# One table of experts' rows for all blocks: 17 whole tiles, then 22 of the other rows

## The chip, the core and the metric

The kernel runs on one core of a Trainium2 chip, as one launch. Its engines each have their own queue of instructions: TensorE (PE; its weight loads are PEld), VectorE (DVE), ScalarE (ACT), GpSimd (POOL) and SyncE (SP), which here issues transfers. They meet only in semaphores. The metric is the device time of a whole execution in microseconds.

## What is computed

A decoder layer in float32 over 32 sequences of 64 tokens with 256 features, in three parts, each added to its input after a layer norm: self-attention, cross-attention to a context, and a feed-forward layer of experts. The last is what the change is about (routing is computed on the normalized input):

```
probs = softmax(x @ Wr)                      # 2048 tokens, 8 experts
topk_w, topk_idx = top_k(probs, 2)
topk_w = topk_w / sum(topk_w)
for i in range(8):
    w_i = sum(topk_w * (topk_idx == i))
    h = silu(x @ Wg[i]) * (x @ Wu[i])        # 256 -> 256
    output = output + w_i * (h @ Wd[i])      # 256 -> 256
```

## The kernel before

Every engine has one Python function that writes its instructions in order (`tensor`, `vector`, `scalar`, `gpsimd`, `sync`). The self-attention runs in eight chunks by a table of due times; cross-attention in four blocks of 512 tokens. Neither is changed, but the routing of a block is done inside the work of the next one, and the routing of the last block (3) inside the expert stage.

Experts are computed only for the rows that chose them. There are 2 x 2048 rows (a token goes to two experts). Each normalized token row is written twice by an indirect transfer on GpSimd (`scatter`, eight for each block, line 1832) into a table in memory, `slots`, at expert base + position within the expert. The table is filled before with rows that name an unused place. Then tiles of 128 rows are read back (`load`, SP, line 1944), one expert each. A tile step i does this:

- TensorE: `gate_up(i)` (six products of 512 columns, three per half of the features, since each float32 is split in a high and a low part), `h_T(i-1)` (transposes of the gated product), `down(i-2)` (six of 256 columns), `x_T(i+2)` (transposes of the tile after next), and then the step's part of the routing, if any.
- VectorE: `gated(i)` writes gu (line 1458), `h_low(i-1)` writes thl (1462), `x_low(i+2)` writes txl (1445), `places(i+2)` writes place (1453), the rows of the results to write to; then the routing's part, the table's part or a `combine`.
- ScalarE: `silu(i)` writes sg, `h_high(i-1)` thh, `copy_out(i-2)` ys, `x_high(i+2)` txh.
- GpSimd: `store(i)` writes ys by an indirect transfer to `results` (line 1866).
- SP: `load(i+6)`; later `results_load(t)`, which brings the two result rows of 128 tokens to gb (line 1953), and `result`, which writes the output.

`h_T(i)` waits for gu of tile i and for thl of tile i-1, `gate_up(i)` for txl of tile i. There are four buffers xs for tiles, six ys and four gb.

The number of tiles is fixed when the kernel is built, for the worst case of a routing. Blocks 0 to 2 have a table of their own: 3072 rows, 24 tiles and up to 7 more since each expert's last tile may be part full, 31. Block 3 has the other: 8 + 7 = 15. From the counts per expert VectorE works out, on all partitions alike, which expert and which first row each tile has (`table_ends`, `table_rows`, lines 1289 to 1311): compare the tile number with the running ends, sum the gaps passed. TensorE and SP read these numbers into registers, eight tiles at a time.

The routing of block 3 stands in the tile steps given by `ROUTE_LAST`: statistics in step 0, normalizing in 2, transposes in 4, logits and maximum in 6, exponential in 8, rank in 9 and 10, choice in 11, shares in 12, positions in 13, slots in 14. The second table follows in steps 15 and 16, and tile 31 is the first that needs it. The combines (two instructions on VectorE for 128 tokens, line 1469) of the first 12 token tiles need the results of all 31 tiles and stand from step 38 on, one a step.

## Times and profile before

| | |
|---|---|
| median of three runs | 696.07 us (695.46 to 696.71) |
| the profiled execution | span 694.2 us from its first to its last instruction; its own run time is not given separately |
| TensorE busy | 636.9 us (92% of the span) |
| VectorE, ScalarE, GpSimd busy | 501.9, 349.2, 256.0 us |
| chain that ended last, by engine | TensorE 79%, ScalarE 8%, VectorE 8%, issue 3%, DMA 2% |
| stores of expert tiles on GpSimd | 46, of 965 ns each |
| loads of tiles, of results | 46 of 129 KB, 16 of 256 KB |
| fill of the two tables | 13416 and 5160 KB, landing after 53.5 and 61.5 us |
| expert stage | gated products from 557.6 to 676.7 us |
| TensorE's granted clock from 560 to 680 us | 1.00 |

The chain is followed back from the last instruction: at each step to what released it. What stands on it costs time; an engine that is busy beside it costs none. "Idle before" of an instruction is in square brackets in a timeline, with what ended it.

### The profile page before, as it was taken

The page shows a single profiled execution, that of the slowest core. Times are in us where ns is not written, and L with a number is a line of the kernel's source. Part 1 is how long each engine was busy: PE and PEld are TensorE (multiplying, and loading weights), DVE is VectorE, ACT ScalarE, POOL GpSimd, SP SyncE. Part 2 cuts the span into 40 slices and gives each one's busy share as a digit, 9 for nine tenths or more (in the row PEclk, how much of TensorE's full clock was granted, in tenths as well). Part 3 has the DMA queues.
Part 4 walks back from the last instruction along what each step waited for, and adds up shares of the span by engine and source line. Part 5 has one row for each costly group of instructions (what it writes and reads, how often), then busy time and mean ns, then how long its engine had stood idle before and what let it go on. Part 6 is the DMA issues. An engine that isn't in the chain of part 4 may idle for free.

```text
span 694.2 us, 15360 instructions
## 1 busy us (share of the span) xinstructions
PE 636.9 (92%) x5650; PEld 474.0 (68%) x5650; DVE 501.9 (72%) x1210; ACT 349.2 (50%) x1207; POOL 256.0 (37%) x233
## 2 busy tenths in 40 slices
PE   3787999998899999999999999999989899999991
PEld 2456777777778667675676766776746688888881
DVE  4998989997468786647986488864788865745585
ACT  1367989997581115721267012670337755455550
POOL 2104000000005744733366642765436322454331
PEclk9998999997799999999999999999998999999996
DMA  8699990000000000000000300003045123344467
GB/s 289 165 373 304 333 319 2 2 2 2 1 1 17 16 1 3 1 16 1 1 2 1 101 23 1 2 10 100 0 149 165 54 77 89 111 124 130 132 195 244
DMA packets 42008, 61.77 MB, mean 89 GB/s; under 512 B 15280, under 2 KB 36272, under 8 KB 41328
## 3 DMA queue, kind: packets, MB, share of 16 engines
q1 hardware_dynamic: 36528, 49.23, 23.7%
q0 software_dynamic: 3744, 10.26, 4.0%
q10 hardware_dynamic: 1664, 1.31, 0.7%
q8 instruction: 46, 0.75, 0.5%
q14 instruction: 26, 0.21, 0.1%
HBM read 48.44 MB, written 31.38 MB: 115 GB/s over the span
## 4 chain that ended last, share of the span: by engine, by line
PE 79%; ACT 8%; DVE 8%; issue 3%; DMA 2%; POOL 0%; ACTq 0%; another core or an unknown queue 0%; SPq 0%; POOLq 0%; DVEq 0%
PE bank L362 68%; PE bank L371 11%; ACT kbd L1546 2%; DMA lncol<-in_L_attn_ln_kv_b 1%; ACT vbd L1532 1%; DVE wlo L1403 1%; ACT ex L1556 1%; ACT xth L1512 1%; DMA gb<-results 1%; ACT ex L1672 1%; DVE m L1122 0%; DMA results<-ys,place 0%; DVE xhat L1362 0%; DVE x L1469 0%; ACT wbh L1602 0%
## 5 line engine op out<-in xcount | busy, mean ns | idle before, releaser
L1122 DVE TENSOR_TENSOR m<-bank,cst 128x512 f32<-128x512 f32 x192 | 122.0, 684 | 38.4 <-PE bank L362 37.1
L1818 POOL TENSOR_TENSOR r<-m,m 128x512 f32<-128x512 f32 x80 | 104.5, 1330 | 114.5 <-DVE m L1122 95.1
L1672 ACT ACTIVATE ex<-bank,nmax 128x64 f32<-128x64 f32 x256 | 73.1, 338 | 27.3 <-DVE nmax L1369 27.3
L362 PE MATMUL bank<-xth,wbh 128*128 128x512 f32 x192 | 79.9, 416 | 1.1 <-DVE m L1122 1.1
L362 PE MATMUL bank<-xth,wbl 128*128 128x512 f32 x192 | 75.2, 392 | 0.0
L362 PE MATMUL bank<-xtl,wbh 128*128 128x512 f32 x192 | 75.1, 391 | 0.0
L1655 ACT ACTIVATE qc<-bank 128x512 f32<-128x512 f32 x32 | 17.4, 595 | 102.6 <-PE bank L362 102.6
L1866 POOL DMA_INDIRECT results<-ys,place x46 | 44.4, 965 | 64.1 <-ACT ys L1745 57.3
L362 PE MATMUL bank<-wop,qc 128*128 128x256 f32 x256 | 62.5, 389 | 0.0
L362 PE MATMUL bank<-r,wqk 64*64 64x512 f32 x512 | 57.7, 594 | 0.0
L362 PEld LDWEIGHTS bank<-wop,qc 128*128 128x128 f32 x256 | 46.4, 189 | 15.2 <-issue 8.8
L1556 ACT ACTIVATE ex<-bank,nmax 128x64 f32<-128x64 f32 x256 | 54.3, 360 | 1.6 <-DVE nmax L1024 1.5
L1672 ACT ACTIVATION_READ_ACCUMULATOR ex<-bank,nmax 128x1 f32 x216 | 49.6, 230 | 0.0
L362 PEld LDWEIGHTS bank<-xth,wbh 128*128 128x128 f32 x192 | 36.0, 188 | 19.0 <-issue 10.1
L1783 POOL TENSOR_TENSOR x<-x,borow 128x512 f32<-128x512 f32 x8 | 10.1, 1270 | 104.9 <-DVE xhat L956 79.4
L1838 POOL TENSOR_TENSOR ex<-ex,inv 128x512 f32<-128x512 f32 x32 | 33.4, 1044 | 41.0 <-DVE inv L1379 40.6
L371 PE MATMUL bank<-cst,ex 128*128 128x128 f32 x256 | 42.6, 291 | 5.8 <-ACT ex L1556 3.3
L371 PEld LDWEIGHTS bank<-cst,ex 128*128 128x128 f32 x256 | 30.2, 147 | 19.1 <-issue 8.8
L362 PEld LDWEIGHTS bank<-xth,wbl 128*128 128x128 f32 x192 | 36.0, 188 | 8.1
L362 PE MATMUL bank<-whi,txh 128*128 x92 | 40.3, 438 | 1.0 <-DVE wlo L1403 1.0
L362 PEld LDWEIGHTS bank<-xtl,wbh 128*128 128x128 f32 x192 | 36.1, 188 | 6.4
L362 PEld LDWEIGHTS bank<-r,wqk 64*64 64x64 f32 x512 | 18.7, 133 | 31.7 <-issue 31.7
(222 smaller groups left out, 1492.1 us busy)
## 6 DMA issues: line engine op xcount, KB each, us to landing
slots<-in_fill SPq DMA_DIRECT2D x1, 13416.0 KB, 53.5
xs<-slots SPq DMA_DIRECT2D x46, 129.0 KB
slots<-in_fill SPq DMA_DIRECT2D x1, 5160.0 KB, 61.5
gb<-results SPq DMA_DIRECT2D x16, 256.0 KB
wo_s<-in_L_xattn_Wo SPq DMA_DIRECT2D x1, 2048.0 KB, 18.6
wq_s<-in_L_xattn_Wq SPq DMA_DIRECT2D x1, 2048.0 KB, 11.8
wraw<-in_L_ffn_Wg SPq DMA_DIRECT2D x8, 256.0 KB, 3.8
wraw<-in_L_ffn_Wu SPq DMA_DIRECT2D x8, 256.0 KB, 3.9
```

Source lines behind the costliest of these rows:

```text
L362: return e.matmul(o, l, r, start=start, stop=stop, skip_group_check=True)
L371: last = e.transpose(o, i, ident)
L1122: last = e.tensor_tensor(m4[n % 2][m][:, :].rearrange("p (b s) -> p b s", s=S), products[half][:, :].rearrange("p (b s) -> p b s", s=S), t ...
L1403: e.tensor_tensor(wlo[:, at], wraw[:, at], whi[:, at].bitcast(F32), ALU.subtract).then_inc(w_lo, 1)
L1546: last = e.activation(kbd[p2][:, :, 2 * t:2 * t + 2, 64 * h2:64 * h2 + 64], bank[0][:, 256:512].rearrange("p (t b l) -> p t b l", t=2, b=2 ...
L1556: last = e.activation(ex[u][:, h * 64:(h + 1) * 64], bank[3 + u % 2][:, h * 64:(h + 1) * 64], ACT.Exp, bias=nmax[u][:, h:h + 1], scale=1.0)
L1655: e.activation(qc[:, 2 * g + pair, :], latent_banks(blk, g)[pair][:, :], ACT.Copy).then_inc(c_qb, 1)
L1672: last = e.activation(ex[b % 4][:, h * 64:(h + 1) * 64], score_banks(b)[odd][:, n * 64:(n + 1) * 64], ACT.Exp, bias=nmax[b % 4][:, 4 * odd ...
L1783: e.tensor_tensor(two, two, borow[:, :].rearrange("p (o d) -> p o d", o=1).broadcast_to([P, 2, D]), ALU.add).then_inc(s_xb, 1)
L1818: last = e.tensor_tensor(rope[n % 6][half][:, :], m4[n % 2][first][:, :], m4[n % 2][second][:, :], op)
L1838: e.tensor_tensor(segments(ex[b % 4]), segments(ex[b % 4]), per_head(inv[b % 2]), ALU.mult).then_inc(c_exn, 1)
L1866: e.indirect_dma_start(out=results[:, :], out_offset=bass.IndirectOffsetOnAxis(ap=place[:, i:i + 1], axis=0), in_=ys[i % YS][:, :], in_off ...
```

## The change

All four blocks now share one table with 2048 rows of room for each expert. After block 2 only whole tiles are certain to be complete: 3072 rows of which at most 127 for each expert are left over, at least 17 whole tiles. These 17 are the first part. What remains of the first three blocks and all of block 3 are the second part of 22 tiles, with 16 entries (expert and blocks) instead of 8; the tiles of the early entries come first in it, so the first three blocks' rows are complete after 31 tiles (`EARLY_DONE`), as before. Together 39 tiles. The routing of block 3 has to be done before tile 17, so it stands in steps 0 to 8, its tables in steps 9 and 10, its scatters in front of stores 7 to 10, two each. Combines begin at step 35, two a step. The constants in SBUF grow (`le` 64 to 256 columns, `next` 16 new, `ebase` 16 to 8, `fill` 12 to 22, `iota` 31 to 22). The table of rows in memory has 17408 rows in place of 13312 + 5120.

```diff
 WE = 2 * KD * F + KF * D
-PARTS_OF = ((0, 3), (3, 4))
-CAP = [4 * P * (hi - lo) for lo, hi in PARTS_OF]
-TILES = [2 * c // P + E - 1 for c in CAP]
+EARLY = 3
+CAP = NT * P
+WHOLE = -(-(2 * 4 * P * EARLY - E * (P - 1)) // P)
+TILES = [WHOLE, 2 * NT + E - 1 - WHOLE]
 FIRST = [0, TILES[0]]
 COLS = [0, -(-TILES[0] // 8) * 8]
+EARLY_DONE = (2 * 4 * P * EARLY + E * (P - 1)) // P
 YS = 6
-ROWS = [-(-(E * c + (E - 1) * P) // 512) * 512 for c in CAP]
+ROWS = -(-(E * CAP + (E - 1) * P) // 512) * 512
...
         RK = 26
+        TAB = 7
         ROUTE_AT = {"stats": 6, "norm": 7, "T": 9, "logits": 10, "max": 10, "exp": 11, "rank": 11, "pos": 12, "slots": 13}
         AHEAD = 6
-        ROUTE_LAST = {"stats": 0, "norm": 2, "T": 4, "logits": 6, "max": 6, "exp": 8, "rank": 9, "pos": 13, "slots": 14}
-        RANK_PARTS = 4
-        COMBINE_AT = TILES[0] + 7
+        ROUTE_LAST = {"stats": 0, "norm": 1, "T": 2, "logits": 3, "max": 3, "exp": 4, "rank": 5, "pos": 7, "slots": 8}
+        LAST_SCATTERS = {7: (0, 1), 8: (2, 3), 9: (4, 5), 10: (6, 7)}
+        COMBINE_AT = EARLY_DONE + 4
...
-                if b in (0, 3):
+                if b == 0:
...
+                n = CAP // P
+                count = pos_bank(b)[:, 64:64 + E].rearrange("p (n o) -> p n o", o=1)
+                if b == EARLY - 1:
+                    e.tensor_tensor(whole[:, :, :], count.broadcast_to([P, E, EARLY * 4]), in_tiles(C("fill")[:, 1:1 + EARLY * 4], E), ALU.is_ge)
+                e.tensor_tensor(full[:, :, :], count.broadcast_to([P, E, n]), in_tiles(C("fill")[:, 0:n], E), ALU.is_gt).then_inc(r_route, 1)
...
+            def early_table():
+                n = TILES[0]
+                w.wait_ge(r_route, RK * EARLY)
+                e.tensor_reduce(nwhole[:, :], whole[:, :, :], AX, ALU.add)
+                e.memset(starts[:, 2 * E:2 * E + 1], float(E * CAP))
+                e.tensor_reduce(early[:, :], full[:, :, :], AX, ALU.add).then_inc(r_tab, 1)
+                w.wait_ge(r_tab, 1)
+                e.tensor_scalar(gap[:, 0:E], nwhole[:, :], -float(P), float(CAP), ALU.mult, ALU.add)
+                e.scalar_tensor_tensor(starts[:, E:2 * E], early[:, :], float(P), C("ebase"), ALU.mult, ALU.add)
+                upto_of(nwhole[:, :], E)
...
+                past_of(n, E)
+                w.wait_ge(r_tab, 4)
+                e.tensor_copy(used[:, 0:1], taken[:, 0:1])
+                e.tensor_tensor(used[:, 1:E], taken[:, 1:E], taken[:, 0:E - 1], ALU.subtract)
+                e.tensor_scalar(own[:, 0:n], C("iota")[:, 0:n], float(P), C("part"), ALU.mult, ALU.add)
+                e.tensor_reduce(expert[:, 0:n], past[:, 0:n, 0:E], AX, ALU.add)
...
+                e.tensor_tensor(own[:, 0:n], own[:, 0:n], rowf[:, 0:n], ALU.add)
+                e.tensor_tensor(row[:, 0:n], C("fill")[:, 0:n], rowf[:, 0:n], ALU.add).then_inc(r_tab, 1)
+                w.wait_ge(r_tab, TAB)
+                e.drain().then_inc(r_table, 1)
+
+            def late_ends():
+                w.wait_ge(r_route, RK * 4)
+                w.wait_ge(r_tab, TAB)
+                e.tensor_reduce(early[:, :], full[:, :, :], AX, ALU.add).then_inc(r_tab, 1)
+                w.wait_ge(r_tab, TAB + 1)
+                e.scalar_tensor_tensor(stops[:, E:2 * E], early[:, :], float(P), C("ebase"), ALU.mult, ALU.add).then_inc(r_tab, 1)
+                w.wait_ge(r_tab, TAB + 2)
+                e.tensor_tensor(spans[:, E:2 * E], stops[:, E:2 * E], starts[:, E:2 * E], ALU.subtract)
+                e.tensor_tensor(gap[:, :], starts[:, 1:2 * E + 1], stops[:, :], ALU.subtract).then_inc(r_tab, 1)
+                w.wait_ge(r_tab, TAB + 3)
+                e.tensor_scalar(spans[:, E:2 * E], spans[:, E:2 * E], 1.0 / P, None, ALU.mult).then_inc(r_tab, 1)
+                w.wait_ge(r_tab, TAB + 4)
+                upto_of(spans[:, :], 2 * E)
+                w.wait_ge(r_tab, TAB + 5)
                 e.tensor_reduce(ends[:, :], upto[:, :, :], AX, ALU.add).then_inc(r_tab, 1)
-                w.wait_ge(r_tab, at + 3)
-                number = C("iota")[:, 0:n].rearrange("p (n o) -> p n o", o=1).broadcast_to([P, n, E])
-                e.tensor_tensor(past[:, 0:n, :], number, in_tiles(ends[:, :], n), ALU.is_ge).then_inc(r_tab, 1)
-
-            def table_rows(q):
-                n, at = TILES[q], 10 * q
-                mine = slice(FIRST[q], FIRST[q] + n)
-                w.wait_ge(r_tab, at + 4)
-                e.tensor_scalar(own[:, mine], C("iota")[:, 0:n], float(P), C("part"), ALU.mult, ALU.add)
-                e.tensor_reduce(expert[:, 0:n], past[:, 0:n, :], AX, ALU.add)
-                e.tensor_tensor(pastgap[:, 0:n, :], past[:, 0:n, :], in_tiles(gap[:, :], n), ALU.mult).then_inc(r_tab, 1)
-                w.wait_ge(r_tab, at + 5)
-                e.tensor_scalar(eoff[:, COLS[q]:COLS[q] + n], expert[:, 0:n], float(E - 1), float(WE), ALU.min, ALU.mult)
-                e.tensor_reduce(rowf[:, 0:n], pastgap[:, 0:n, :], AX, ALU.add).then_inc(r_tab, 1)
-                w.wait_ge(r_tab, at + 6)
-                e.tensor_tensor(own[:, mine], own[:, mine], rowf[:, 0:n], ALU.add).then_inc(r_tab, 1)
-                e.scalar_tensor_tensor(row[:, COLS[q]:COLS[q] + n], C("iota")[:, 0:n], float(P), rowf[:, 0:n], ALU.mult, ALU.add).then_inc(r_tab, 3)
-                w.wait_ge(r_tab, at + 10)
+                w.wait_ge(r_tab, TAB + 6)
+                past_of(TILES[1], 2 * E)
+            def late_rows():
+                n, cols = TILES[1], slice(COLS[1], COLS[1] + TILES[1])
+                mine = slice(FIRST[1], FIRST[1] + n)
+                w.wait_ge(r_tab, TAB + 7)
+                e.tensor_scalar(own[:, mine], C("iota"), float(P), C("part"), ALU.mult, ALU.add)
+                e.tensor_tensor(pastnext[:, :, :], past[:, :, :], in_tiles(C("next"), n), ALU.mult)
+                e.tensor_tensor(pastgap[:, :, :], past[:, :, :], in_tiles(gap[:, :], n), ALU.mult).then_inc(r_tab, 1)
+                w.wait_ge(r_tab, TAB + 8)
+                e.tensor_reduce(expert[:, :], pastnext[:, :, :], AX, ALU.add)
+                e.tensor_reduce(rowf[:, :], pastgap[:, :, :], AX, ALU.add).then_inc(r_tab, 1)
+                w.wait_ge(r_tab, TAB + 9)
+                e.tensor_scalar(eoff[:, cols], expert[:, :], float(WE), None, ALU.mult)
+                e.scalar_tensor_tensor(own[:, mine], rowf[:, :], starts[:, 0:1], own[:, mine], ALU.add, ALU.add)
+                e.scalar_tensor_tensor(row[:, cols], rowf[:, :], starts[:, 0:1], C("fill"), ALU.add, ALU.add).then_inc(r_tab, 1)
...
+                    rank_sum(b)
                 elif b == 3 and n == at["rank"] + 1:
-                    rank_sum(b)
-                elif b == 3 and n == at["rank"] + 2:
                     rank_chosen(b)
-                elif b == 3 and n == at["rank"] + 3:
                     rank_shares(b)
...
-                    table_ends(1)
+                    late_ends()
-                    table_rows(1)
+                    late_rows()
                 if i >= COMBINE_AT:
-                    combine(i - COMBINE_AT)
-            for t in range(tiles + 2 - COMBINE_AT, NT):
+                    for t in range(2 * (i - COMBINE_AT), 2 * (i - COMBINE_AT) + 2):
+                        combine(t)
+            for t in range(2 * (tiles + 2 - COMBINE_AT), NT):
                 combine(t)
...
-                t, half = divmod(i - ROUTE_LAST["slots"], 3)
-                if 0 <= t < 4 and half < 2:
+                for n in LAST_SCATTERS.get(i, ()):
                     w.wait_ge(t_hT, i + 2)
-                    scatter(3, 2 * t + half)
+                    scatter(3, n)
                 store(i)
...
-            for n, d in enumerate(slots):
-                rows = a["fill"][sum(ROWS[:n]):sum(ROWS[:n + 1]), :]
-                e.dma_start(d.rearrange("(p n r) d -> p n (r d)", p=P, r=4), rows.rearrange("(p n r) d -> p n (r d)", p=P, r=4)).then_inc(d_fill, 16)
+            e.dma_start(slots.rearrange("(p n r) d -> p n (r d)", p=P, r=4), a["fill"].rearrange("(p n r) d -> p n (r d)", p=P, r=4)).then_inc(d_fill, 16)
...
-                w.wait_ge(d_scat, 128 * PARTS_OF[q][1])
+                w.wait_ge(d_scat, 128 * (EARLY, 4)[q])
                 if i in RUNS:
-                    at.update(zip(RUNS[i], load_run(e, row, RUNS[i], ROWS[q] - P)))
-                e.dma_start(xs[i % 4][:, :], slots[q][bass.ds(at[i], P), :]).then_inc(d_xs[i % 4], 16)
+                    at.update(zip(RUNS[i], load_run(e, row, RUNS[i], ROWS - P)))
+                e.dma_start(xs[i % 4][:, :], slots[bass.ds(at[i], P), :]).then_inc(d_xs[i % 4], 16)
...
-                done = TILES[0] if t < 12 else sum(TILES)
+                done = EARLY_DONE if t < 4 * EARLY else sum(TILES)
...
-                if 0 <= i - COMBINE_AT + 3 < 12:
-                    results_load(i - COMBINE_AT + 3)
-                if i == COMBINE_AT + 6:
-                    result(0, 4)
+            for t in range(8):
+                results_load(t)
+            result(0, 4)
+            for t in range(8, 12):
+                results_load(t)
             result(4, 8)
```

VectorE around the rank of block 3, before (gu, thl, txl and place are the four instructions of a tile step, cmpa, cmpb and rank the comparison of experts):

```order
L1462 TENSOR_TENSOR thl_210<-bank,thh_208 128x256
L1445 TENSOR_TENSOR txl_203<-bank,txh_200 128x256
L1453 SCALAR_TENSOR_TENSOR place<-xs_197,own 128x1
L1217 TENSOR_TENSOR cmpa<-ew 128x256
L1218 TENSOR_TENSOR cmpb<-ew 128x256
L1220 TENSOR_TENSOR cmpb<-cmpb,cst 128x256
L1458 TENSOR_TENSOR gu_206<-bank,sg_204 128x256
L1462 TENSOR_TENSOR thl_211<-bank,thh_209 128x256
L1445 TENSOR_TENSOR txl_201<-bank,txh_198 128x256
L1453 SCALAR_TENSOR_TENSOR place<-xs_194,own 128x1
L1225 TENSOR_TENSOR cmpa<-cmpa,cmpb 128x256
L1227 TENSOR_REDUCE rank<-cmpa 128x32
```

and now:

```order
L1502 TENSOR_TENSOR txl_210<-bank,txh_207 128x256
L1510 SCALAR_TENSOR_TENSOR place<-xs_205,own 128x1
L1232 TENSOR_TENSOR cmpa<-ew 128x256
L1233 TENSOR_TENSOR cmpb<-ew 128x256
L1235 TENSOR_TENSOR cmpb<-cmpb,cst 128x256
L1240 TENSOR_TENSOR cmpa<-cmpa,cmpb 128x256
L1242 TENSOR_REDUCE rank<-cmpa 128x32
L1515 TENSOR_TENSOR gu_214<-bank,sg_212 128x256
L1519 TENSOR_TENSOR thl_219<-bank,thh_217 128x256
L1502 TENSOR_TENSOR txl_211<-bank,txh_208 128x256
L1510 SCALAR_TENSOR_TENSOR place<-xs_202,own 128x1
L1247 TENSOR_SCALAR chosen<-rank 128x32
```

The five instructions of the rank, which had the four of a step between them, are now in one step, and the choice follows in the next.

GpSimd, the stores of tiles 13 to 19 before, with the scatters of block 3 between them:

```order
L1866 DMA results<-ys1_213,place_157 22529x256
L1832 DMA slots1<-mxhat_145,index_139 5120x258
L1866 DMA results<-ys2_214,place_157 22529x256
L1832 DMA slots1<-mxhat_145,index_139 5120x258
L1866 DMA results<-ys3_215,place_157 22529x256
L1866 DMA results<-ys4_216,place_157 22529x256
L1832 DMA slots1<-mxhat_145,index_139 5120x258
L1866 DMA results<-ys5_217,place_157 22529x256
L1832 DMA slots1<-mxhat_145,index_139 5120x258
L1866 DMA results<-ys0_212,place_157 22529x256
```

and now, stores of tiles 6 to 12:

```order
L1923 DMA results<-ys0_220,place_165 21505x256
L1889 DMA slots<-mxhat_144,index_138 17408x258 x2
L1923 DMA results<-ys1_221,place_165 21505x256
L1889 DMA slots<-mxhat_144,index_138 17408x258 x2
L1923 DMA results<-ys2_222,place_165 21505x256
L1889 DMA slots<-mxhat_144,index_138 17408x258 x2
L1923 DMA results<-ys3_223,place_165 21505x256
L1889 DMA slots<-mxhat_144,index_138 17408x258 x2
L1923 DMA results<-ys4_224,place_165 21505x256
L1923 DMA results<-ys5_225,place_165 21505x256
```

The eight scatters stood one at a time in front of two stores out of three; now two stand in front of each of four stores, seven tiles earlier.

VectorE in the last steps before, x being the combine of one token tile (the last thl is the last row):

```order
L1458 TENSOR_TENSOR gu1_207<-bank,sg1_205 128x256
L1462 TENSOR_TENSOR thl0_210<-bank,thh0_208 128x256
L1445 TENSOR_TENSOR txl0_201<-bank,txh0_198 128x256
L1453 SCALAR_TENSOR_TENSOR place_157<-xs1_195,own_156 128x1
L1469 SCALAR_TENSOR_TENSOR x_49<-gb1_219,share_140,x_49 128x256 x2
L1458 TENSOR_TENSOR gu0_206<-bank,sg0_204 128x256
L1462 TENSOR_TENSOR thl1_211<-bank,thh1_209 128x256
L1469 SCALAR_TENSOR_TENSOR x_49<-gb2_220,share_140,x_49 128x256 x2
L1458 TENSOR_TENSOR gu1_207<-bank,sg1_205 128x256
L1462 TENSOR_TENSOR thl0_210<-bank,thh0_208 128x256
L1469 SCALAR_TENSOR_TENSOR x_49<-gb3_221,share_140,x_49 128x256 x2
L1462 TENSOR_TENSOR thl1_211<-bank,thh1_209 128x256
```

and now:

```order
L1526 SCALAR_TENSOR_TENSOR x_49<-gb2_228,share_139,x_49 128x256 x2
L1526 SCALAR_TENSOR_TENSOR x_49<-gb3_229,share_139,x_49 128x256 x2
L1515 TENSOR_TENSOR gu1_215<-bank,sg1_213 128x256
L1519 TENSOR_TENSOR thl0_218<-bank,thh0_216 128x256
L1526 SCALAR_TENSOR_TENSOR x_49<-gb0_226,share_139,x_49 128x256 x2
L1526 SCALAR_TENSOR_TENSOR x_49<-gb1_227,share_139,x_49 128x256 x2
L1515 TENSOR_TENSOR gu0_214<-bank,sg0_212 128x256
L1519 TENSOR_TENSOR thl1_219<-bank,thh1_217 128x256
L1526 SCALAR_TENSOR_TENSOR x_49<-gb2_228,share_139,x_49 128x256 x2
L1526 SCALAR_TENSOR_TENSOR x_49<-gb3_229,share_139,x_49 128x256 x2
L1519 TENSOR_TENSOR thl0_218<-bank,thh0_216 128x256
L1526 SCALAR_TENSOR_TENSOR x_49<-gb0_226,share_139,x_49 128x256 x2
```

Two combines stand where one stood, and they start closer to the last tile.

## Rows read from the trace of the kernel before

**Rows 1.** The chain that ended last, by line, from the page

```profile
PE bank L362 68%; PE bank L371 11%; ACT kbd L1546 2%; DMA lncol<-in_L_attn_ln_kv_b 1%; ACT vbd L1532 1%; DVE wlo L1403 1%; ACT ex L1556 1%; ACT xth L1512 1%; DMA gb<-results 1%; ACT ex L1672 1%; DVE m L1122 0%; DMA results<-ys,place 0%; DVE xhat L1362 0%; DVE x L1469 0%; ACT wbh L1602 0%
```

**Rows 2.** Timeline of VectorE and TensorE in undisturbed tile steps (start us, us, engine, line)

```profile
633.51 0.43 DVE L1458 TENSOR_TENSOR gu<-bank,sg 128x256 f32<-128x256 f32 x1 [0.79 <-ACT sg L1735]
656.45 0.43 DVE L1458 TENSOR_TENSOR gu<-bank,sg 128x256 f32<-128x256 f32 x1 [0.78 <-ACT sg L1735]
657.65 0.42 DVE L1445 TENSOR_TENSOR txl<-bank,txh 128x256 fp32r<-128x256 f32 x1 [0.45 <-ACT txh L1730]
657.99 0.21 DVE L1453 SCALAR_TENSOR_TENSOR place<-xs,own 128x1 uint32<-128x1 f32 x1
658.38 0.38 PE L371 MATMUL bank<-cst,gu 128*128 128x128 f32 x2
```

**Rows 3.** Issues of transfers: bytes and us to landing

```profile
cst<-in_constants ACTq DMA_DIRECT2D x1, 763.0 KB, 4.7
```

**Rows 4.** Timeline, first table on VectorE, and GpSimd beside it

```profile
532.89 1.24 DVE L1291 TENSOR_TENSOR upto<-cst,ntile 128x64 f32<-128x64 f32 x1
532.99 1.05 POOL L1838 TENSOR_TENSOR ex<-ex,inv 128x512 f32<-128x512 f32 x1
```

**Rows 5.** Timeline of GpSimd, VectorE and TensorE, steps 0 to 3

```profile
560.51 1.04 POOL L1825 TENSOR_TENSOR mrstd<-mvar,cst 128x4 f32<-128x4 f32 x1 [15.74 <-DVE mvar L1194]
563.54 1.46 DVE L1201 TENSOR_SCALAR mxhat<-x,mmv,mrstd 128x256 f32<-128x256 f32 x4
562.32 0.48 PE L362 MATMUL bank<-whi,txh 128*128 x1
```

**Rows 6.** Timeline of ScalarE and TensorE around the exponential of step 8

```profile
580.96 1.28 ACT L1704 ACT_TABLE_LOAD   x1
582.50 1.28 ACT L1735 ACT_TABLE_LOAD   x1
585.11 0.41 PE L371 MATMUL bank<-cst,gu 128*128 128x128 f32 x2 [0.71 <-DVE thl L1462]
```

**Rows 7.** Timeline of VectorE, rank and chosen, steps 9 to 11

```profile
585.50 0.43 DVE L1217 TENSOR_TENSOR cmpa<-ew 128x256 f32<-128x256 f32 x1
586.66 0.42 DVE L1458 TENSOR_TENSOR gu<-bank,sg 128x256 f32<-128x256 f32 x1
589.97 0.19 DVE L1232 TENSOR_SCALAR chosen<-rank 128x32 f32<-128x32 f32 x1
591.07 0.42 DVE L1458 TENSOR_TENSOR gu<-bank,sg 128x256 f32<-128x256 f32 x1
```

**Rows 8.** Timeline of VectorE, second table, step 15 and gu of 16

```profile
600.82 0.25 DVE L1278 TENSOR_TENSOR full<-bank,cst 128x96 f32<-128x96 f32 x1
602.30 0.41 DVE L1458 TENSOR_TENSOR gu<-bank,sg 128x256 f32<-128x256 f32 x1
```

**Rows 9.** Timeline of GpSimd and of SP's queue, the last scatter before

```profile
629.45 0.96 POOL L1832 DMA_INDIRECT slots<-mxhat,index  x1 [0.98 <-PE bank L371]
630.72 0.96 POOL L1866 DMA_INDIRECT results<-ys,place  x1 [0.30 <-DVE place L1453]
632.95 0.93 SPq L1944 DMA_DIRECT2D xs<-slots  x2
```

**Rows 10.** Timeline of VectorE, the first combine

```profile
660.67 1.00 DVE L1469 SCALAR_TENSOR_TENSOR x<-gb,share,x 128x256 f32<-128x256 f32 x2
661.65 0.42 DVE L1458 TENSOR_TENSOR gu<-bank,sg 128x256 f32<-128x256 f32 x1
```

**Rows 11.** Timeline of the end: GpSimd, SP's queue, VectorE

```profile
681.19 1.16 POOL L1866 DMA_INDIRECT results<-ys,place  x1 [0.32 <-issue]
684.49 1.82 SPq L1953 DMA_DIRECT2D gb<-results  x4
687.44 1.01 DVE L1469 SCALAR_TENSOR_TENSOR x<-gb,share,x 128x256 f32<-128x256 f32 x2 [4.09 <-DMA gb<-results]
```

**Rows 12.** Timeline of GpSimd, a scatter of block 2

```profile
542.43 2.34 POOL L1832 DMA_INDIRECT slots<-mxhat,index  x1 [0.17 <-issue]
```

88 lines of the change are left out of this document (52 added, 36 removed).

## The prediction

> **What bounds the kernel now.** I read the chain of waits first, as a sum by line [rows 1]. Matmuls and transposes of TensorE make 79% of it; small shares belong to `wlo` on VectorE, to the `gb<-results` loads at the end and to a parameter load at the start. So a microsecond of TensorE work taken off is a microsecond gained, unless something else comes late. The expert stage is 46 tile steps in a row. From one gated product on VectorE to the one nine steps on takes 22.94 us [rows 2], 2.549 us a step, and TensorE has no gap in it. VectorE has four instructions in such a step: gu at 656.45 and thl behind it, then 0.45 us of idleness, txl at 657.65 and place at 657.99, done at 658.12. The next gu could start at 656.45 + 2.55 = 659.00. Route work, table work and combines stand behind place, so 0.88 us of them is free in a step, and 1.33 us if the 0.45 is used up too. TensorE asks for gu and thl in its transposes at 658.38, 1.93 us after gu starts; gu and thl need 0.76 us and a signal. A gu may therefore be about 1.1 us late before TensorE stalls. I call what it is late at a step's start L. A load R behind place gives L = R - 0.88 from rest, and L + R - 1.33 when VectorE is late already; what exceeds 1.1 is a stall.
>
> **What is removed.** 46 tiles become 39. Seven steps of 2.549 us are -17.8 us. All other instructions of TensorE stay: the routing's transposes, logits and position products, five register loads for the runs of tiles (before at tiles 8, 16, 24, 31, 39, now at 8, 16, 17, 25, 33).
>
> **Start and first table.** The constants grow by 192 + 16 - 8 + 10 - 9 = 201 columns, about 100 KB on 763 KB. That load took 4.7 us to land [rows 3]; parameter loads that the chain passes through [rows 1] stand behind it in the same queue. At its own rate 100 KB are 0.6 us; other loads run beside it, so between 0 and 0.6, I take 0.3. The fill becomes one transfer 3% smaller and nothing waits for its end: 0.
> The early table on VectorE grows from 12 instructions to 21, with one more reduction, and stands on the chain. Against that its four large ones shrink from 248 to 136 columns, about 0.12 us each. What counts is the wait in the middle: `upto` took 1.24 us, till 534.13, and GpSimd's product ran from 532.99 to 534.04 [rows 4]. The extra reduction falls into that wait. Behind it nine small ones of about 0.09 us make +0.8 against -0.5. I take +0.1, between -0.3 and +0.8.
> The Trainium skill (SBUF — State Buffer, Who interferes with whom) says that a VectorE instruction with two SBUF inputs contends with a GpSimd instruction that reads SBUF, one of them being held for the whole of the other. The trace agrees, by those two rows: the held instruction ends 0.09 us after GpSimd's. By the rule the new two-input instruction waits in the same place and the sum is +0.1; without it the extra reduction would come on top, +0.3.
>
> **Routing, steps 0 to 8.** The statistics stay in step 0. The four normalizing instructions move to step 1. They need mrstd, ready at 561.55, and take 1.46 us, so they end at about 563.05. The transposes of the routed block now stand at the end of TensorE's step 2, which is over at 562.32 [rows 5]. Stall 0.8 us (0.3 to 1.0); before, two steps lay between.
> The exponential at step 4 costs two table loads of 1.28 us as it did at step 8, and TensorE's stall of 0.71 there stays [rows 6]: 0.
> Rank at step 5 is now five instructions of 256 columns in a row. Three took 1.16 us (585.50 to gu at 586.66) [rows 7]; with the other two it is about 2.1. Right behind the late silu VectorE has no slack: gu of step 6 comes 0.9 us later than its counterpart did, where TensorE had almost none to give (gu at 586.66 with thl is over by 587.4, wanted by about 587.7). Stall 0.7. At step 6 chosen (589.97 to 591.07, 1.1 us) and shares (five more of that kind, 0.6) stand together, and TensorE wants their result for the positions at the end of its step 7. It gets there about 1.15 us (thl, txl, place) + 1.7 us after gu of step 6, that is 1.0 us after TensorE is through. Together 1.7 us (0.5 to 2.5).
>
> **Second table and the wait for tile 17.** This replaces a queue with room by one without. Count and ends (step 9) took 1.48 us, 600.82 to 602.30 [rows 8]. Now there are nine instructions, `past` has 352 columns for 120 and `upto` 256 for 64: at about 1 ns a column +0.23 (past), +0.2 and +0.2 (upto and its sum), three more dependent small ones +0.6: 2.7 us. The rows part (step 10) has four instructions of 352 columns and four small ones, 2.2 us. L after step 9 is 2.7 - 0.88 = 1.8, stall 0.7; after step 10, 1.1 + 2.2 - 1.33 = 2.0, stall 0.9. So 1.6 us by the table.
> Meanwhile GpSimd has the eight scatters of the last block between four stores, two ahead of each. Spacing of two such instructions is 1.27 us [rows 9]. From the first scatter to the end of the last are eleven instructions: 10 x 1.27 + 0.96 = 13.7 us. The end of the last scatter of before (630.41) and the load that waited for it (632.95) are 2.54 us apart [rows 9]. The load itself took no more than 2.95 us where it had twice the bytes [rows 11]; I take 2.1. Tile 17 is in SBUF 18.3 us after the first scatter. That scatter can start when the indices are there, at the end of step 8, and after store 6, both about 0.4 us past the nominal gu of step 9. TensorE wants tile 17 at the end of step 15, 6 x 2.549 + 1.6 = 16.9 us past that. Wait 18.3 + 0.4 - 16.9 - 0.3 (the end of step 15 lies 0.3 past its gu) = 1.5 us. Table and wait are one account: 3.1 us. If the table costs less, the wait grows by as much. Bounds 1.0 (spacing as measured, load hidden) and 5.5. What is behind the waiting load on SP are only tiles 18 to 38. Before, there was no such wait: the scatters were spread over twelve steps and tile 31 was wanted late enough.
>
> **The end.** Combines of twelve token tiles start at step 35, two a step, where before one a step started at 38. One costs 0.98 us (660.67 to gu at 661.65) [rows 10]. From the start of the first, VectorE has eight combines, 7.9 us, and gu, thl, txl, place of three steps, 2.5 us, before the last thl: 10.4 us. The first starts 0.88 before the nominal gu of step 36, so the last thl starts 9.5 us past it. Undisturbed, as before, it lies two shorter last steps and 1.8 us further, 6.7. So 2.8 us late; the last store had 0.7 us of GpSimd's queue before it, which is then gone. The last store is 2.1 us later against the last tile than it was. Four combines remain, 3.9 us, over before that store has landed (3.1 us after its start) [rows 11] by about a microsecond, so SP's `result(8, 12)` is no new hold. The rest, four loads and four combines, is as it was. I take +2.1 us, between +0.5 (TensorE's stalls before this stretch leave VectorE ahead and the backlog is short) and +4.5 (the loads hold VectorE too, once for every pair).
>
> **Sum.** -17.8 + 0.3 + 0.1 + 0.8 + 1.7 + 3.1 + 2.1 = -9.7 us. The profiled execution's span 694.2 becomes 684.5. The median of the runs, 696.07, lies 1.9 above that span; the same on top gives 686.4 us.
>
> **Rivals.** A: the stalls hide in one another. TensorE waiting for tile 17 lets VectorE catch up and the routing stalls are half of mine. For it: what was late in step 9 of before cost only 0.71. Then -17.8 + 4.5 = -13.3, 682.8. Against: the queue's 13.7 us are hard.
> B: more is given back. Loads of results hold VectorE in the last steps, and the wait for tile 17 is 3 us. -17.8 + 12.5, 690.8. For it: two loads of 256 KB per step, with only four buffers. Against: 2.95 us to land is within the time between use and reuse.
> C, slower than before: a scatter's descriptors take longer beside dense VectorE work. One of before took 2.34 us instead of 0.96 next to `wlo` on VectorE [rows 12]. Eleven in a row at 1.38 us more each are 15.2 us more ahead of tile 17, 701.6. It decides from 0.96 + 9.7 / 11 = 1.8 us apiece. Against: in the expert stage they took 0.96 also beside table work.
> The Trainium skill (SBUF — State Buffer, SBUF: two separate sides) has this as the trap that VectorE in a two-port mode keeps GpSimd from writing descriptors. By it these scatters would be late wherever copies stand beside them; the 0.96 us of this stage speaks against it here.
> D: the change does not do what it says. More tiles than 39 would run, or the 17 are waited for as late as the 22. GpSimd's order shows 39 stores, so only a wait is open: tile 17 seven steps late, 17.8 us, and no change, 696.
>
> **Chances.** Forecast 0.60, A 0.18, B 0.16, C 0.04, D 0.02. For the range: below 681.5 lies a tenth, above 690.5 another. Two measurements of this kernel can be told apart from about 0.2%, 1.4 us. Faster by more: 0.95; within: 0.01; slower: 0.04. The forecast's own range is 684 to 689.
>
> **What would show it.** TensorE's transposes of the routed block wait about 0.8 us in step 2; the positions product waits about 1 us; txh of tile 17 is idle before it, with SP waiting for the last scatter; last thl comes about 2.8 us late; last store lands 3.1 us after its start. No wait at tile 17 means that my count of GpSimd's queue is wrong. A wait of over 3 us there, or scatters over 1.8 us each, are C.

## The result and the profile after

The changed kernel takes 691.28 us (689.99 to 692.59, five runs) against 696.71 beside it: ratio 0.9922, 95% interval 0.9895 to 0.995. It is faster by 5.4 us; 9.7 were forecast. 691.28 lies 2.3 above the forecast's own range (684 to 689) and 0.8 above 690.5, over which the prediction had put a tenth. All ratios are of fast executions; the only slow one is one of four of x13, with 1198.37 us. The profiled execution has a span of 689.3 us, 4.9 less than before, where the sum said 684.5.

The page of the profile: the chain by line, which answers to [rows 1], and the load of the constants, which answers to [rows 3].

```profile
PE bank L377 64%; PE bank L386 10%; ACT kbd L1604 2%; DMA lncol<-in_L_attn_ln_kv_b 1%; DVE x L1526 1%; ACT vbd L1590 1%; DVE wlo L1460 1%; ACT ex L1614 1%; ACT xth L1570 1%; DMA gb<-results 1%; ACT ex L1730 1%; DVE txl L1502 0%; DVE m L1137 0%; DVE xhat L1419 0%
...
cst<-in_constants ACTq DMA_DIRECT2D x1, 863.5 KB, 5.0
```

TensorE's two lines make 74% of the chain now, 79% before; VectorE has 11% for 8%. The rows answering to [rows 5 to 8]: TensorE's waits in steps 1 to 12, in brackets (start us, us, engine, line; idle time before, and what ended it).

```profile
562.61 0.41 PE L386 MATMUL bank<-cst,gu 128*128 128x128 f32 x2 [0.62 <-DVE thl L1519]
564.41 1.09 PE L386 MATMUL bank<-cst,mxhat 128*128 128x128 f32 x8 [0.47 <-DVE mxhat L1216]
577.03 0.41 PE L386 MATMUL bank<-cst,gu 128*128 128x128 f32 x2 [0.73 <-DVE thl L1519]
580.37 0.41 PE L386 MATMUL bank<-cst,gu 128*128 128x128 f32 x2 [0.49 <-DVE thl L1519]
582.52 0.41 PE L377 MATMUL bank<-chosen,cst 128*128 128x32 f32 x2 [0.81 <-DVE share L1271]
593.42 0.41 PE L386 MATMUL bank<-cst,gu 128*128 128x128 f32 x2 [0.86 <-DVE thl L1519]
597.36 0.41 PE L386 MATMUL bank<-cst,gu 128*128 128x128 f32 x2 [1.20 <-DVE gu L1515]
601.55 0.66 PE L386 MATMUL bank<-cst,xs 128*128 128x128 f32 x2 [3.08 <-DVE txl L1502]
```

The ones at 564.41, 577.03, 580.37 and 582.52 were expected: normalizing, exponential, rank, positions. 593.42 and 597.36 stand behind the second table's two halves. The 3.08 us at 601.55 are not the wait for tile 17: these are the transposes of tile 14, and they wait for txl of tile 13, which waited for ScalarE:

```profile
591.76 0.39 ACT L1788 ACTIVATE txh<-bank 128x256 fp32r<-128x256 f32 x1 [0.41 <-PE bank L386]
595.38 0.39 ACT L1793 ACTIVATE sg<-bank 128x256 f32<-128x256 f32 x1 [3.24 <-remote]
599.12 0.38 ACT L1803 ACTIVATE ys<-bank 128x256 f32<-128x256 f32 x1 [2.57 <-PE bank L377]
600.56 0.39 ACT L1788 ACTIVATE txh<-bank 128x256 fp32r<-128x256 f32 x1 [1.05 <-remote]
602.07 0.39 ACT L1793 ACTIVATE sg<-bank 128x256 f32<-128x256 f32 x1 [1.13 <-remote]
594.00 1.58 POOL L1889 DMA_INDIRECT slots<-mxhat,index  x1 [0.30 <-issue]
```

The last row is a scatter beside it. "remote" says that the profile knows no releaser: no instruction that raises the awaited semaphore had ended shortly before. The trace records when a semaphore was raised, and that tells more. I set the end of TensorE's product (a modelled time), the moment at which TensorE's semaphore for it was raised, and the start of the ScalarE instruction that waits for it beside one another (us):

| ScalarE | product ended | semaphore raised | ScalarE started |
|---|---|---|---|
| sg, an undisturbed step | 587.47 | 587.49 | 587.51 |
| sg | 592.56 | 595.36 | 595.38 |
| thh | 593.83 | 596.14 | 596.16 |
| ys | 594.53 | 599.10 | 599.12 |
| txh | 594.75 | 600.54 | 600.56 |
| sg | 596.16 | 602.05 | 602.07 |

ScalarE started 0.02 us behind each signal, as in an undisturbed step. What came late is TensorE's signal, by 2.3 to 5.9 us. So where the expectations below and this text say that ScalarE is late or held, it waits for a signal of TensorE; I had read the first profile otherwise. Of the recorded signals between gu of the first and of the last tile, 8 of TensorE's 129 came over 0.3 us late, and none of VectorE's 175 or of ScalarE's 132. GpSimd's scatter at 602.36, which waits for a TensorE signal too, came late with them. TensorE's later products go on starting at their usual spacing meanwhile; whether a product or only its signal was late, the modelled ends cannot tell.

In the stretch between, TensorE idles, and its granted clock falls, from 1.00 to a half (2.4 to 1.2 GHz):

```profile
602.50:605.22 2.72, 2.72 (x12) 0.61 0.19 67
605.22:661.14 55.92, 55.92 (x355) 1.00 0.37 115
```

The end answers to [rows 10, 11]: thl three times late, products at half clock, the last store and the loads behind it.

```profile
668.88 0.41 PE L386 MATMUL bank<-cst,gu 128*128 128x128 f32 x2 [0.63 <-DVE thl L1519]
671.57 0.41 PE L386 MATMUL bank<-cst,gu 128*128 128x128 f32 x2 [1.58 <-DVE thl L1519]
673.92 0.58 PE L377 MATMUL bank<-whi,thh 128*128 x1 [1.24 <-DVE thl L1519]
674.29 0.42 PE L377 MATMUL bank<-wlo,thh 128*128 x1
676.74 1.13 POOL L1923 DMA_INDIRECT results<-ys,place  x1 [1.92 <-ACT ys L1803]
679.44 2.21 SPq L2007 DMA_DIRECT2D gb<-results  x4
682.84 4.33 DVE L1526 SCALAR_TENSOR_TENSOR x<-gb,share,x 128x256 f32<-128x256 f32 x8 [4.17 <-DMA gb<-results]
```

TensorE waits 0.63, 1.58 and 1.24 us; its last products take 0.41 us each, where the same took 0.28 earlier.

To compare executions I divide the expert stage at the starts of gu of tiles 0, 8, 17 and the last but three (35). Such starts are single rows, as 558.99 for gu 0 in the changed kernel. "Signal" is the longest time from the end of a TensorE product to its signal to ScalarE. Times in us:

| execution | gu 0 at | 0 to 8 | 8 to 17 | 17 to 35 | 35 to end | span | signal |
|---|---|---|---|---|---|---|---|
| undisturbed steps of 2.541 | | 20.3 | 22.9 | 45.74 | | | 0.02 |
| changed kernel | 558.99 | 26.40 | 30.00 | 45.75 | 28.16 | 689.3 | 5.9 |
| x5, x9 (the same again) | 560.57, 559.16 | 26.39 | 30.04, 30.33 | 45.75 | 27.65, 27.98 | 690.4, 689.6 | 5.7, 5.8 |
| x16 (the same again) | 559.68 | 26.39 | 31.39 | 45.74 | 27.90 | 691.1 | 4.4 |
| x4 (the same again) | 558.52 | 26.40 | 29.21 | 45.74 | 28.03 | 687.9 | 0.02 |
| x1 no scatters | 556.14 | 26.39 | 25.08 | 45.74 | 28.45 | 681.8 | 0.02 |
| x13 plain writes | 559.11 | 26.41 | 25.07 | 45.74 | 28.47 | 684.8 | 0.02 |
| x10 48 more on ScalarE | 557.75 | 26.41 | 30.26 | 45.74 | 28.05 | 688.2 | 5.8 |
| x11 half the scatters | 559.86 | 26.41 | 25.30 | 45.74 | 29.49 | 686.8 | 2.1 |
| x6 scatters in one piece | 560.72 | 26.40 | 33.23 | 45.74 | 28.71 | 694.8 | 8.5 |
| x14 scatters over six stores | 558.66 | 26.41 | 34.42 | 45.74 | 28.17 | 693.4 | 3.3 |
| x2 table in four steps | 558.77 | 26.49 | 29.11 | 45.75 | 28.08 | 688.2 | 0.02 |
| x3 one combine a step | 559.19 | 26.40 | 27.27 | 45.75 | 30.49 | 689.1 | 0.02 |
| x7 that, and SP's order | 560.90 | 26.40 | 30.28 | 45.76 | 27.06 | 690.4 | 5.8 |
| x12 table, positions, tail | 559.50 | 24.92 | 29.62 | 45.74 | 26.62 | 686.4 | 4.2 |
| x8 x12 with x6 | 558.74 | 24.86 | 34.07 | 45.73 | 26.70 | 690.1 | 8.9 |
| x15 x12 with x14 | 559.35 | 24.94 | 33.61 | 45.74 | 26.56 | 690.2 | 3.5 |

Two of the columns, 0 to 8 and 17 to 35, repeat to 0.1 us between executions and chips wherever the code is the same. What varies is when the stage begins (556.1 to 560.9 in programs that are the same up to there), what happens from tile 8 to tile 17, and by less the end. The kernel before has late signals too, beside its scatters: 16, by up to 1.8 us.

### The profile page after: what moved, and what is told of

The parts are those of the page before. It is cut to its first block, busy times and chain, and to the rows that moved or that the text cites. A ratio compares the mean times of both kernels' runs of the same rounds, so it can differ in the third digit from the quotient of the medians.

```text
span 689.3 us, 14960 instructions
## 1 busy us (share of the span) xinstructions
PE 621.6 (90%) x5538; PEld 459.4 (67%) x5538; DVE 496.2 (72%) x1196; ACT 341.1 (49%) x1179; POOL 250.2 (36%) x226
## 4 chain that ended last, share of the span: by engine, by line
PE 74%; DVE 11%; ACT 8%; issue 4%; DMA 2%; another core or an unknown queue 1%; ACTq 0%; POOL 0%; SPq 0%; POOLq 0%; DVEq 0%
PE bank L377 64%; PE bank L386 10%; ACT kbd L1604 2%; DMA lncol<-in_L_attn_ln_kv_b 1%; DVE x L1526 1%; ACT vbd L1590 1%; DVE wlo L1460 1%; ACT ex L1614 1%; ACT xth L1570 1%; DMA gb<-results 1%; ACT ex L1730 1%; DVE txl L1502 0%; DVE m L1137 0%; DVE xhat L1419 0%
## 5 line engine op out<-in xcount | busy, mean ns | idle before, releaser
L1923 POOL DMA_INDIRECT results<-ys,place x39 | 37.8, 968 | 65.0 <-ACT ys L1803 63.0
L377 PEld LDWEIGHTS bank<-wop,qc 128*128 128x128 f32 x256 | 46.4, 189 | 15.6 <-issue 9.2
L1515 DVE TENSOR_TENSOR gu<-bank,sg 128x256 f32<-128x256 f32 x39 | 16.5, 423 | 29.0 <-ACT sg L1793 27.2
```

Source lines behind the costliest of these rows:

```text
L377: return e.matmul(o, l, r, start=start, stop=stop, skip_group_check=True)
L1515: e.tensor_tensor(gu[i % 2][:, :], bank[1 + i % 2][:, F:2 * F], sg[i % 2][:, :], ALU.mult).then_inc(t_gu, 1)
L1923: e.indirect_dma_start(out=results[:, :], out_offset=bass.IndirectOffsetOnAxis(ap=place[:, i:i + 1], axis=0), in_=ys[i % YS][:, :], in_off ...
```

## The experiments

The experiments stand in four groups, each measured on a chip of its own: x1 to x4, x5 to x8, x9 to x12, x13 to x16. Ratios are to the kernel before on the same chip, with the 95% interval in brackets. A run is best compared with the changed kernel in its own group: x4, x5, x9 and x16. The cuts of code leave out what only follows: where scatters are left out, the load of tile 17 no longer waits for them either.

**x1, no scatters.**

```diff
-                for n in LAST_SCATTERS.get(i, ()):
-                    w.wait_ge(t_hT, i + 2)
-                    scatter(3, n)
```

> The changed kernel without the eight scatters of block 3 (they are left out, and the last four combines read the results of tokens 0 to 511 instead, so the output is not the reference's; tile steps, tables and combines are the same). In the changed kernel ScalarE came late by itself in steps 11 to 13: it started sg at 595.38 where its operand was ready at about 592.6, ys at 599.12 (ready 594.4), txh at 600.56, sg at 602.07, and TensorE then waited 3.08 us and had its clock at 0.57. Theory Q (GpSimd's dense queue of scatters holds ScalarE up, by their descriptors or their traffic): without scatters ScalarE has no such wait, TensorE's 3.08 us and the slow clock behind it go, about 4.5 us: 686.8. Theory V (VectorE's late table of 13 wide instructions in two steps holds ScalarE up): the wait stays, 691. Theory I (ScalarE's own instructions arrive late at that place, whatever the others do): the wait stays at the same instruction, 691. My prediction's theory (tile 17 comes late by the scatters' queue) expects 1.5 us less, 689.8.

Measured 684.28 us, ratio 0.9883 (0.9854 to 0.9912). ScalarE has no late stretch, TensorE no wait but those of the table:

```profile
590.33 0.41 PE L386 MATMUL bank<-cst,gu 128*128 128x128 f32 x2 [0.62 <-DVE thl L1519]
594.26 0.41 PE L386 MATMUL bank<-cst,gu 128*128 128x128 f32 x2 [1.19 <-DVE thl L1519]
```

From 8 to 17 it takes 25.08, so the table alone costs 2.2 us. It is tempting to call theory Q shown, but this chip had no late signal with scatters either: in x2, x3 and x4 they were all within 0.02 us. What the edit took away here is the wait for tile 17, and the slow clock behind it where there was one: 27.27 us (x3) and 29.21 (x4) became 25.08. On Q, V and I this run says nothing; x11 and x13 do, beside x9 and x16. (The stage also begins 2.4 us earlier than in x4, which the edit cannot explain.)

**x2, the second table in four steps.**

```diff
                if i == ROUTE_LAST["slots"] + 1: route_count(3); late_ends()
-               if i == ROUTE_LAST["slots"] + 2: late_rows()
+               if i == ROUTE_LAST["slots"] + 2: late_upto()
+               if i == ROUTE_LAST["slots"] + 3: late_rows()
+               if i == ROUTE_LAST["slots"] + 4: late_sums()
```

> The second table in four steps (9 to 12) in place of two, same instructions. In the changed kernel TensorE waited 0.86 us (step 10's gu late behind the ends) and 1.20 us (step 11's behind the rows), in all 2.1, and then 3.08 us for ScalarE. Theory of the prediction (table and wait for tile 17 are one account): the 2.1 us go but tile 17, whose data wait for the last scatter, then holds TensorE for as much: 690 to 691. Theory V (dense VectorE work holds ScalarE): ScalarE's late stretch goes as well, 2.1 + 4.4 less, of which tile 17 takes back about 3: 687 to 688. Theory Q and I: 2.1 less, the late stretch of ScalarE stays and hides tile 17: 689.2.

Measured 690.0, ratio 0.9954 (0.9928 to 0.9979). The table's two waits are gone, and in their place:

```profile
607.09 0.69 PE L386 MATMUL bank<-cst,xs 128*128 128x128 f32 x2 [3.58 <-DMA xs<-slots]
608.00:610.00 2.00, 2.00 (x6) 0.50 0.51 152
```

This is my wait for tile 17, "<-DMA xs<-slots", with the half clock behind it. ScalarE was not late on this chip. The prediction's "one account" holds here: with the table faster, tile 17 takes it back (29.11 from 8 to 17, in x4 29.21).

**x3, one combine in a step.**

```diff
-                    for t in range(2 * (i - COMBINE_AT), 2 * (i - COMBINE_AT) + 2):
-                        combine(t)
-            for t in range(2 * (tiles + 2 - COMBINE_AT), NT):
+                    combine(i - COMBINE_AT)
+            for t in range(tiles + 2 - COMBINE_AT, NT):
```

> One combine in each step from 35 on in place of two; all others follow the last thl. In the changed kernel TensorE waits 0.63, 1.58 and 1.24 us for thl in the last three steps and its last six products run at clock 0.5, 0.41 us for 0.28. Theory of the prediction (the pairs of combines are what makes the last thl late): these waits go, and the last store comes 3 to 4 us earlier; the six combines that are left over take 6 us behind the last thl, before the last store has landed: 687.5 to 688.5. Rival (the combines moved behind the last step hold SP's loads of results, which wait for buffers): 691, no gain. Up to step 35 this is the changed kernel again: if ScalarE is late in steps 11 to 13 here too, at the same instruction, it is no accident of one execution.

Measured 690.28, ratio 0.9946 (0.9924 to 0.9969): no gain on x4's 689.63. Both halves of the expectation show. The last store comes at 670.50, 11.9 us behind gu 35 in place of 15.6; but SP's queue reads:

```profile
669.15 3.65 SPq L2006 DMA_DIRECT2D gb<-results  x4
672.84 6.17 SPq L2012 DMA_DIRECT2D out<-x  x2
679.24 2.31 SPq L2006 DMA_DIRECT2D gb<-results  x4
```

The write of token tiles 8 to 11, the second of the pair at 672.84, waits for combine 11, which ends at 678.6, and the loads for the last four combines stand behind it. The rival was right on the sum, the prediction's theory on the cause of the late thl. Up to step 35 this was the changed kernel, here with the wait for tile 17 and no fall of the clock:

```profile
607.70 0.44 PE L386 MATMUL bank<-cst,xs 128*128 128x128 f32 x2 [1.40 <-DMA xs<-slots]
605.59 4.10 SPq L1997 DMA_DIRECT2D xs<-slots  x5
602.00:610.00 8.00, 6.51 (x39) 1.00 0.52 164
```

**x4, empty instructions on ScalarE.**

```diff
+                for _ in range(48 if blk == 1 else 0):
+                    e.nop()
```

> 48 empty instructions on ScalarE early in the second block of cross-attention, where it waits for TensorE; they shift every later instruction of ScalarE by 48 places in its stream and nothing else. Theory I (ScalarE's instructions are late at a certain place of its stream): its late stretch, now at 592 to 602, moves to another tile step or goes; the time changes by 0 to -4.5 us. Theories Q and V: the stretch stays in steps 11 to 13, and the time within 0.3% of 691.3.

The trace holds 14960 instructions, as without; whether the empty ones are missing in the program or only in the record, it does not show. And on this chip no signal was late with or without them, so x4 tells nothing of theory I. I take it as the changed kernel again: 689.63, ratio 0.9938 (0.9918 to 0.9958). It does price the clock. Here TensorE waited 1.82 us for tile 17, in x3 1.40:

```profile
607.44 0.44 PE L386 MATMUL bank<-cst,xs 128*128 128x128 f32 x2 [1.82 <-DMA xs<-slots]
609.21 0.63 PE L377 MATMUL bank<-wlo,txh 128*128 x1
602.00:610.00 8.00, 6.15 (x33) 0.91 0.51 165
610.00:618.00 8.00, 8.00 (x47) 0.87 0.28 82
```

Wait and products together: 29.21 us from 8 to 17 against 27.27. A wait 0.4 us longer goes with 1.9 more, since the clock fell. That rests on this one pair of executions.

**x5, the changed kernel again.** No edit.

> The changed kernel itself once more, beside the others on the same chip. In the profiles of x2, x3 and x4 ScalarE was not late in steps 11 to 13, and the wait of TensorE was for the load of tile 17 instead (1.40, 1.82 and 3.58 us before its transposes). Theory of an accident: here too TensorE waits for tile 17, 1.4 to 1.9 us, and from gu of step 8 to gu of step 17 it takes 27.3 us without and 29.2 us with a fall of the clock behind that wait, where 22.9 would be undisturbed. If ScalarE's stretch belongs to the kernel, it shows again at 592 to 602. Ratio to the kernel before 0.992.

692.59, ratio 0.9946 (0.992 to 0.9972). ScalarE's ys had waited 4.64 us at 600.46, TensorE waited 2.87 behind it, and nothing for tile 17. So the lateness is no accident of one execution, and the first theory falls: on the chip of x2 to x4 the wait was tile 17's, on the three others, as x5, x9 and x16 show, the late signals'.

**x6, all eight scatters before store 7.**

```diff
-        LAST_SCATTERS = {7: (0, 1), 8: (2, 3), 9: (4, 5), 10: (6, 7)}
+        LAST_SCATTERS = {7: range(8)}
```

> All eight scatters of block 3 in front of store 7, in place of two in front of each of stores 7 to 10. The last scatter then ends 8 x 1.27 = 10.2 us after the first starts, not 14 to 15. Theory K (tile 17 waits for GpSimd's queue, and the clock falls behind a long wait): the wait for tile 17 goes, and the slow products behind it: gu 8 to gu 17 takes 25.1 us (as without scatters), 2.2 to 4.2 less than the changed kernel beside it. Rival R (the stores behind the scatters are now late, ys runs out of buffers, or the tile is late for another reason, such as its load or the table): gu 8 to gu 17 stays at 27 to 29.

694.28, ratio 0.9983 (0.9956 to 1.001): slower than x5 beside it, and neither theory. TensorE does not wait for tile 17, and its signals are later than ever, by up to 8.5 us:

```profile
602.79 0.38 ACT L1803 ACTIVATE ys<-bank 128x256 f32<-128x256 f32 x1 [6.04 <-remote]
604.92 0.38 ACT L1788 ACTIVATE txh<-bank 128x256 fp32r<-128x256 f32 x1 [1.75 <-remote]
605.91 0.45 PE L386 MATMUL bank<-cst,xs 128*128 128x128 f32 x1 [5.73 <-DVE txl L1502]
```

ys at 602.79 started 0.02 us behind TensorE's signal (602.77), so rival R's missing buffer is not what it waited for.

**x7, one combine a step, and the loads ahead of the write.** The edit of x3, and in SP's queue:

```diff
             result(4, 8)
-            result(8, 12)
             for t in range(12, NT):
                 results_load(t)
+            result(8, 12)
```

> One combine in each step from 35 on, as in x3, and SP loads the results of token tiles 12 to 15 before it writes tokens tiles 8 to 11. In x3 the last store was 6 us earlier than in the changed kernel but these loads were issued at 679.24, 7.6 us after it, since SP stood at the write that waits for combine 11. Theory (the pairs of combines delay TensorE and the last store, and x3 lost it again in SP's order): the loads start with combine 8 to 11, the last combine starts about 4 us earlier than in x3, and from gu 35 to the end it takes 26.5 us for 28.2 in the changed kernel and 30.5 in x3. Rival (VectorE's 16 combines behind the last gu are what sets the end, in whatever order): 28 or more.

690.18, ratio 0.9905 (0.9869 to 0.994), 2.4 us under x5 beside it. From 35 to the end 27.06 (x5: 27.65), not 26.5. The chain of waits says why (start us, us, what):

```profile
675.21 5.46 DMA results<-ys,place
680.78 3.06 DMA gb<-results
```

and of the changed kernel:

```profile
676.74 2.58 DMA results<-ys,place
```

The last store, at 675.21, took 5.46 us to land beside the loads of four results, issued from 673.87 on. In the changed kernel it took 2.58, the last such load issued 2.9 us before it.

**x8, four edits.** x6, x2 and x7 together, and

```diff
-        ROUTE_LAST = {..., "rank": 5, "pos": 7, "slots": 8}
+        ROUTE_LAST = {..., "rank": 5, "pos": 8, "slots": 8}
```

> Four edits together: scatters as in x6, the second table in four steps as in x2, the tail as in x7, and the positions product of block 3 in step 8 in place of 7 (TensorE waited 0.80 us for it in step 7, and its result is wanted by VectorE only at the end of step 8). If the givebacks are separate terms: 0.8 (positions), 2.1 (table), 2 to 4 (tile 17 and clock), 1.7 (tail), in all 6.6 to 8.6 us below the changed kernel beside it, ratio to the kernel before 0.981. If they stand in for one another (tile 17 becomes late again as soon as the rest is faster): 3 to 4 us below, 0.987.

692.2, ratio 0.9946 (0.9918 to 0.9973). Against x5 nothing: 8 to 17 takes 34.07 with the scatters in one piece (x6: 33.23, x5: 30.04), and that eats the rest. The positions alone brought 1.5 us, 26.4 to 24.9.

**x9, the changed kernel a third time.** No edit.

> The changed kernel once more, the measure for the three beside it. On two chips ScalarE was late in steps 11 to 13 (ys or sg 4.6 to 6.1 us late, only with the scatters), on a third it was not, in three programs that were the same up to there (the empty instructions of x4 had not come into the program, which had 14960 instructions as before; it was the changed kernel again). If the lateness belongs to the chip, gu 8 to gu 17 is 29 to 30 us here or 27.3 to 29.2, and the three beside it fall on the same side.

690.96, ratio 0.9933 (0.9909 to 0.9958); 8 to 17 in 30.33. ys waited 6.05 us. The product had ended at 594.69 and its signal came at 600.51; the chain of waits has no name for what lies between (start us, us, what):

```profile
594.12 6.39 another core or an unknown queue
600.51 0.02 issue
600.53 0.07 ACT ys L1803
```

**x10, 48 real instructions on ScalarE.**

```diff
+                    for k in range(4 if blk == 1 and s < 12 else 0):
+                        e.activation(spare[:, 4 * s + k:4 * s + k + 1], C("part"), ACT.Copy)
```

> 48 small real activations (128x1, into a buffer of their own that nobody reads) on ScalarE in the second block of cross-attention, four in each of twelve places where it has room, so every later instruction of ScalarE stands 48 places further in its stream. Theory I (its instructions arrive late at one place of the stream while the scatters load the transfer engines): where the third run of the changed kernel shows ScalarE late at about its activation 1066, the late one here is about 48 activations earlier, that is before the scatters, and so does not show; gu 8 to gu 17 27.3 us. Theory Q (the scatters hold ScalarE, wherever its stream is): late in steps 11 to 13 again, as in the run beside it. If the run beside it shows no lateness, this one tells nothing on it.

691.16, ratio 0.993 (0.9905 to 0.9955). 15008 instructions, 48 more, and yet ScalarE is late in the same steps:

```profile
593.36 0.38 ACT L1796 ACTIVATE sg<-bank 128x256 f32<-128x256 f32 x1 [2.46 <-remote]
599.15 0.38 ACT L1806 ACTIVATE ys<-bank 128x256 f32<-128x256 f32 x1 [3.94 <-remote]
600.41 0.42 PE L387 MATMUL bank<-cst,xs 128*128 128x128 f32 x2 [3.19 <-DVE txl L1503]
```

8 to 17 takes 30.26 (x9: 30.33). Theory I falls, by this and by the signals: wherever ScalarE idled here it started 0.02 us behind TensorE's signal, so its instruction was there and waiting.

**x11, half the scatters.**

```diff
+        LAST_SCATTERS = {7: (0,), 8: (1,), 9: (2,), 10: (3,)}
```

> Four scatters of block 3, one in front of each of stores 7 to 10, in place of eight; the other four are left out and the last four combines read the results of tokens 0 to 511, so the output is not the reference's. The queue of GpSimd is 5 us shorter, so tile 17 has no wait. Theory of density (two scatters and a store in each step are what ScalarE cannot stand): no lateness, gu 8 to gu 17 25.1 us as in x1, which had no scatter. Theory I or a fixed point in time: ScalarE is late by as much as in the run beside it, 27 to 29 us.

687.12, ratio 0.9864 (0.9814 to 0.9914). 8 to 17 in 25.30. TensorE's signals are late once, by up to 2.1 us (sg waits 2.50 at 595.51), where VectorE is late with the table anyway, so it costs 0.2. The theory of density has its number, but x14 will speak against density and for the count.

**x12, x8 with the scatters as in the changed kernel.**

> x8 without its change of the scatters, which in x6 made the kernel 1.7 us slower: the second table in four steps, the positions in step 8, one combine a step and the loads of the last results ahead of the write of tiles 8 to 11. By separate terms: 0.8 (positions), 1.5 to 2 (tail), and of the table's 2.1 nothing, since tile 17 or ScalarE's lateness takes it back: 2.5 us below the changed kernel beside it, ratio to the kernel before 0.989. Rival: x7 (the tail alone) is as good, 0.9905 to 0.992, because wherever TensorE is faster the wait for tile 17 grows by as much.

688.97, ratio 0.9899 (0.9861 to 0.9937), with x9 beside it at 0.9933: about 2 us under the changed kernel, where 2.5 were expected. Its signals are late too (29.62). The rival is not excluded: x7, the tail alone, has 0.9905 on its own chip, and the intervals overlap.

**x13, plain writes in place of the scatters.**

```diff
+                        e.dma_start(spill[n * P:(n + 1) * P, :], mxhat[:, n // 2, :]).then_inc(d_out, 16)
```

> The eight scatters of block 3 are left out and eight plain transfers of the same tiles (128 rows of 1032 bytes) to a table of their own in memory are issued by SP, two ahead of each of the loads of tiles 13 to 16; the last four combines read the results of tokens 0 to 511, so the output is not the reference's. Theory of traffic (ScalarE is late because transfers write the rows): late here too, gu 8 to gu 17 29 to 30 us. Theory of GpSimd (its indirect transfers, 1.27 us apart, hold ScalarE): no lateness, 25.1 to 25.5 us.

688.03, ratio 0.9887 (0.9869 to 0.9905). 25.07 from 8 to 17, and no signal later than 0.02 us; x16, the changed kernel beside it, has 31.39 and signals up to 4.4 us late:

```profile
588.30 0.83 SPq L2020 DMA_DIRECT2D spill<-mxhat  x2
592.86 0.96 SPq L2020 DMA_DIRECT2D spill<-mxhat  x2
593.32 0.41 PE L387 MATMUL bank<-cst,gu 128*128 128x128 f32 x2 [0.62 <-DVE gu L1516]
597.25 0.41 PE L387 MATMUL bank<-cst,gu 128*128 128x128 f32 x2 [1.19 <-DVE thl L1520]
```

The same bytes from the same buffers do no harm, though they go out within 6 us and not within 15. So it is not the bytes. What is left is that GpSimd issues the transfers and that they are indirect, with rows that go to scattered places; no run tells these apart.

**x14, the scatters over six stores.**

```diff
+        LAST_SCATTERS = {7: (0,), 8: (1,), 9: (2, 3), 10: (4,), 11: (5, 6), 12: (7,)}
```

> The eight scatters in front of six stores (1, 1, 2, 1, 2 and 1 in front of stores 7 to 12) in place of four. Theory of density: ScalarE is late by 1 to 2.5 us, as with half of them, in place of 6; but the last scatter starts at about gu 14 and tile 17 then has its own wait of 2 to 3 us, with the clock behind it at 0.5: gu 8 to gu 17 28 to 30 us, within 0.2% of the kernel beside it. Theory that the number of them counts, not their spacing: ScalarE as late as before, and tile 17 behind it: 31 us or more.

695.15, ratio 0.9979 (0.9956 to 1.0001), 2.7 us above x16 beside it; 34.42 from 8 to 17: the theory of number. The signals are late three times, by up to 3.3 us (in x16 by up to 4.4), and tile 17 comes on top:

```profile
594.36 0.39 ACT L1793 ACTIVATE sg<-bank 128x256 f32<-128x256 f32 x1 [2.52 <-remote]
601.93 0.38 ACT L1793 ACTIVATE sg<-bank 128x256 f32<-128x256 f32 x1 [3.09 <-remote]
608.79 0.38 ACT L1793 ACTIVATE sg<-bank 128x256 f32<-128x256 f32 x1 [3.29 <-remote]
611.77 0.69 PE L386 MATMUL bank<-cst,xs 128*128 128x128 f32 x2 [4.85 <-DMA xs<-slots]
```

**x15, x12 with these scatters.**

> x12 (second table in four steps, positions in step 8, tail as in x7) with the scatters as in x14. If spacing relieves ScalarE: gu 8 to gu 17 27.5 us against 29.6 in x12, ratio to the kernel before 0.987. If tile 17 takes it all back: 0.990 as x12 had.

692.01, ratio 0.995 (0.9935 to 0.9966): no better than x16 beside it (692.44), so with the scatters spread x12's gain is gone. Spacing does not relieve ScalarE, and TensorE waits 4.76 us for tile 17.

**x16, the changed kernel a fourth time.** No edit.

> The changed kernel, the measure for the three beside it: 0.992 to 0.995 of the kernel before; gu 8 to gu 17 30.0 to 30.3 us with ScalarE late, or 27.3 to 29.2 on a chip like that of x2 to x4, and then the three beside it tell nothing on ScalarE.

692.44, ratio 0.9947 (0.9931 to 0.9963). 8 to 17 in 31.39, with the late signals and no wait for tile 17.

## Why the prediction was wrong

Its sum gave back 8.1 us of 17.8; 12.9 were given back (17.8 - 4.9, by the two profiled executions). The step that failed is the one on the scatters and the wait for tile 17: it let GpSimd's queue cost time only to what waits for its transfers. The terms measured below make 13.3; most of the steps behind tile 17 were a little shorter than before (2.541 for 2.549). By its steps:

- **Removed tiles: right.** The steps that remain take 2.54 us, 18 of them 45.75.
- **Constants and first table, +0.4: in the profile +1.4, not explained.** The load went from 4.7 to 5.0 us and the first transposes from 9.53 to 9.84, and that 0.3 had vanished by 165 us (165.47 before, 165.45 now). The table cost 0.4 (from the end of its qc to nmax 4.83, now 5.20), for 0.1. VectorE waited beside GpSimd's product again, as [rows 4] had let expect, but not in the instruction that I named: `gap`, with one tensor as input, took from 534.10 to 535.08 (0.16 us before), GpSimd's product ended at 535.05, and `upto` started at 535.08. The rest is drift over the blocks before. Programs that are the same up to there begin the stage anywhere from 556.1 to 560.9, so 1.4 us is within the scatter. (The fill is 5.6% smaller, not 3%; nothing hangs on it.)
- **Routing in steps 0 to 8, +2.5: measured +2.7.** From gu 0 to gu 8 there are 6.1 us over eight plain steps; before, the same routing cost 3.3 from gu 0 to gu 14. The waits were 0.47 for the normalizing (0.8 expected), 0.73 for the exponential (0.71), 0.49 for rank (0.7), 0.81 for positions (1.0). The last was avoidable: the positions may stand a step later at no cost.
- **Second table, +1.6: x1 has 2.2.**
- **Scatters and tile 17, +1.5: this step failed.** On three chips of four and in the first profile they cost 4.9 to 6.3 (30.0 to 31.4 against 25.1; on one chip, x16 against x13, 6.3), of which about 1.2 were already paid before (26.70 us from gu 18 to gu 28 for 25.5). On the fourth chip it was 2.2 and 4.1. There the wait for tile 17 exists and has the forecast size, 1.40 and 1.82 us, and my count of the queue is right: eleven instructions took 13.8 us in x3, where I had 13.7. In the changed kernel's own profile there is no such wait, which I had called a sign of a wrong count; TensorE was late for another reason and the tile was there. Two things were missing. First, such a wait may bring the clock down: +1.9 for 0.4 us more of waiting. Second, I put at nothing what the scatters do beside their own queue. With them in place TensorE's signals to ScalarE came up to 4.4 to 5.9 us late in the changed kernel; with half of them up to 2.1; without them, or with plain writes by SP, never over 0.02. ScalarE's work stands in every step of TensorE's, so TensorE waits for its own late signal. A sign of it was in the trace of before and I had passed over it: ys waited 1.55 us, "remote", at 622.34, right behind a scatter; the product had ended at 620.52, and the signal came at 622.31.
- **The end, +2.1: measured +3.3.** The last thl came 3.1 us late against gu 35 (2.8 expected), but the last products ran at half the clock, 0.41 us each for 0.28, and the last store came 3.7 later (15.6 behind gu 35, before 11.9). The waits for thl are right in size; what the term lacked is the clock behind them. That SP's write of tiles 8 to 11 is "no new hold" held for the changed kernel, and failed by 6 us for x3.

Rival B, with 12.5 given back, came nearest (690.8), but by luck: its reasons were loads of results that hold VectorE and 3 us for tile 17, and in the changed kernel's profile VectorE waits 0.46 us for such loads in the last steps, and no wait for the load of tile 17 shows. Rival C fell: scatters took 0.96 us, but for one of 1.58 and some of 1.14. The harm came beside scatters of normal length. Rivals A and D fell: the stalls did not hide in one another, and tile 17 was not late by seven steps.

The Trainium skill (SBUF — State Buffer, Who interferes with whom) says of the ports of SBUF that TensorE and ScalarE never wait on anyone. The runs do not contradict it: they do not show the ports, and ScalarE's waits here ended 0.02 us behind signals of TensorE. But x13 against x16 shows that these signals come late beside GpSimd's indirect transfers, so the sentence is no reason to count such a neighbour at nothing.

What stays open: how GpSimd's indirect transfers make TensorE's signals late, and only TensorE's. It is not ScalarE's place in its instruction stream (x10), not the bytes (x13), not the spacing (x14). VectorE's table stands unchanged in x13, where no signal is late, so it is not the table by itself. And it stays open why one of the four chips of the experiments did not show it.

## What to carry to other kernels

Price a moved indirect transfer on every engine that works beside it, not only on its own queue: an unexplained wait of another engine behind one in the trace of before is the row to read. When such a wait is "remote", compare three times before naming a culprit: the end of the work it waits for, the moment its semaphore was raised, and the start. Here they moved the fault from ScalarE to TensorE's signal. Check that the run beside an experiment shows the effect on the same chip at all: x1 looked like the answer and was not. Add to a long wait of TensorE what its products may cost at half the clock behind it: here 1.9 us behind one of 1.82, and nothing behind one of 1.40. When iterations are taken out, ask what was hidden in them: here the combines lost seven steps of cover, and moving them behind the end only helps when the transfers in the same queue are put in the order in which they can start.

## What the runs showed of the hardware

- Beside eight indirect transfers of 128 rows by GpSimd, two of them 1.27 us apart, TensorE's semaphores to ScalarE were raised up to 4.4 to 5.9 us after the end of the product, on three of four chips (x5, x9, x16) and in the first profile of the changed kernel; on the fourth (x2 to x4) within 0.02 us. With eight in a row it was 8.5 us (x6), with four 2.1 (x11), with eight plain transfers of the same size by SP 0.02 (x13). In no run was a signal of VectorE or of ScalarE in this stage over 0.3 us late.
- TensorE's granted clock stayed at 1.00 across a wait of 1.40 us for a tile and fell to 0.50 (1.2 GHz) behind one of 1.82 in another execution of the same instructions, for 3.4 us. It did so at every wait of 2.87 us or more between gu of tile 8 and gu of tile 17 in these runs. In x16 it stayed at 1.00 behind a wait of 2.42 us and fell behind one of 2.27, so the length of one wait does not decide it.
- The landing of the last store (128 rows) took 2.58 us where the last load of 256 KB had been issued 2.9 us before it (changed kernel), and 5.46 and 4.25 us beside four such loads (x7, x12).
